# GpSimd's feature add moved behind VectorE's two-operand instructions, with both engines' rounds reordered

## The reference, cut to what matters

```python
xn = layernorm(x)
q, k, v = xn @ Wq, xn @ Wk, xn @ Wv            # 16 heads of 64
q, k = elu(q) + 1, elu(k) + 1
k_sum = k.sum(over the 2048 rows)              # per batch and head
kv = einsum('bhnd,bhne->bhde', k, v)
out = einsum('bhnd,bhde->bhne', q, kv) / (q . k_sum + 1e-6)
x = x + out @ Wo + bo
h = square(relu(layernorm(x) @ W_fc.T)); y = h @ W_proj.T
x = x + (spikes of a 5-step threshold neuron driven by y) / 5
```

## Time and profile before

| | us |
|---|---|
| median of 3 runs | 1173.32 (1172.75 to 1173.76) |
| span of the profiled execution | 1172.8 |
| TensorE busy in it | 1071.5 (91%) |
| VectorE busy | 1027.1 (88%) |
| ScalarE busy | 736.5 (63%) |
| GpSimd busy | 650.7 (55%) |

### The profile page before, as it was taken

One profiled execution on the slowest core, in us unless ns is written; L12 is line 12 of the kernel. 1 busy time (PEld: TensorE's weight loads), 2 busy tenths in 40 slices (PEclk: granted clock), 3 DMA queues, 4 the chain that ended last, 5 costly groups with the idle time before them and its releaser, 6 DMA issues.

```text
span 1172.8 us, 21946 instructions
## 1 busy us (share of the span) xinstructions
PE 1071.5 (91%) x6384; PEld 626.0 (53%) x6384; DVE 1027.1 (88%) x1873; ACT 736.5 (63%) x1219; POOL 650.7 (55%) x390
## 2 busy tenths in 40 slices
PE   5888888888888889898999999999999999999998
PEld 2333333333333337665666666666666666666666
DVE  7888988998898856999999899899899899899976
ACT  5565756665666565557766666666766657666653
POOL 3334333333333434448787768767777677677742
PEclk9999999999999999999999999999999999999999
DMA  3332226225222213444454544434434434434421
GB/s 103 105 89 67 55 70 159 68 55 124 73 67 56 54 45 64 84 92 95 100 105 96 109 90 103 102 85 106 108 81 101 107 90 97 101 91 97 86 54 37
DMA packets 261849, 101.63 MB, mean 87 GB/s; under 512 B 216592, under 2 KB 259728, under 8 KB 261776
## 3 DMA queue, kind: packets, MB, share of 16 engines
q1 hardware_dynamic: 261776, 100.84, 37.4%
HBM read 31.59 MB, written 16.78 MB: 41 GB/s over the span
## 4 chain that ended last, share of the span: by engine, by line
DVE 45%; PE 20%; issue 19%; ACT 15%; DVEq 1%; POOL 0%; ACTq 0%; DMA 0%
DVE xn L833 13%; ACT feat L668 6%; DVE feat L969 6%; ACT feat L666 6%; PE acc L599 5%; PE acc L578 5%; DVE zsum L972 5%; DVE feat L841 4%; PE proj L488 4%; PE acc L565 3%; DVE spikes L944 3%; DVE newt L827 2%; DVE newt L830 2%; ACT xnat L662 2%; DVE newt L824 2%
## 5 line engine op out<-in xcount | busy, mean ns | idle before, releaser
L1037 POOL TENSOR_TENSOR qT<-qT,feat 128x1024 f32<-128x1024 f32 x64 | 151.4, 2366 | 268.7 <-DVE feat L841 268.7
L1057 POOL TENSOR_TENSOR h<-h_f,h 128x512 f16<-128x512 f32 x128 | 145.8, 1160 | 157.0 <-ACT h L775 157.0
L511 PE MATMUL acc<-feat,xnat 128*128 128x512 f16 x768 | 176.9, 380 | 39.8 <-DVE feat L865 39.6
L488 PE MATMUL proj<-xn2T,xT 128*128 128x512 f16 x768 | 178.3, 382 | 33.2 <-DMA xT<-xnat 29.2
L841 DVE SCALAR_TENSOR_TENSOR feat<-proj,feat 128x1024 f32<-128x1024 f32 x128 | 156.4, 1222 | 56.3 <-ACT feat L668 38.4
L1052 POOL TENSOR_TENSOR feat<-feat 128x1024 f16<-128x1024 f32 x64 | 185.7, 2901 | 20.6 <-ACT feat L754 20.6
L599 PE MATMUL acc<-wpT,h 128*128 128x256 f16 x1536 | 181.2, 276 | 12.6 <-DVE spikes L944 12.6
L565 PE MATMUL acc<-m_all,qT 128*128 (+1 forms) x1536 | 179.8, 274 | 4.7 <-DMA qT<-feat 3.4
L662 ACT ACTIVATE xnat<-xn 128x256 f16<-128x256 f32 x128 | 53.2, 416 | 201.5 <-DVE xn L833 201.2
L578 PE MATMUL acc<-xn2T,wfcT 128*128 128x512 f16 x768 | 176.2, 379 | 0.0
L488 PE MATMUL proj<-wq,xT 128*128 128x512 f16 x768 | 176.2, 379 | 0.0
(11 more groups left out here) (56 smaller groups left out, 1337.0 us busy)
## 6 DMA issues: line engine op xcount, KB each, us to landing
x_t<-in_L_attn_x_dram SPq DMA_DIRECT2D x128, 128.0 KB, 2.2
xT_spill<-xT SPq DMA_DIRECT2D x64, 128.0 KB, 1.9
xT<-xT_spill SPq DMA_DIRECT2D x64, 128.0 KB, 2.1
out_dram<-out_t SPq DMA_DIRECT2D x64, 128.0 KB, 1.9
m_all<-in_L_attn_Wk_dram SPq DMA_DIRECT2D x4, 256.0 KB, 4.8
xT<-xnat SPq DMA_TRANSPOSE x64, 2.4
m_all<-in_L_ffn_W_fc_dram SPq DMA_DIRECT2D x4, 256.0 KB, 3.1
wv<-in_L_attn_Wv_dram SPq DMA_DIRECT2D x4, 256.0 KB, 3.3
```

Of the source, the lines that this page charges most:

```text
L488: mm = pe.matmul(proj[:, slot, half * HALF:(half + 1) * HALF], xT[:, u, left * C2 + c2, :], w[:, right, c2, half * HALF:(half + 1) * HALF] ...
L511: mm = pe.matmul(acc[:, c2 * 2 + half, :], xnat[:, u, left, c2 * P:(c2 + 1) * P], feat16[:, u % 2, right, half * HALF:(half + 1) * HALF], ...
L1037: pool.tensor_tensor(kacc[:, b, :], kacc[:, b, :], feat[:, u % 2, :], ALU.add).then_inc(k_added, 1)
L1057: pool.tensor_tensor(h[:, par, LO, f, :], h_f[:, f % 4, :], h[:, par, HI, f, :], ALU.subtract).then_inc(h_lo, 1)
```

## The change

The four parts belong together:

- GpSimd's add of tile n no longer starts when elu n is done. It waits as well for "ln1.lo" of tile n+3, that is for `xn_lo` of VectorE's round n+1.
- VectorE's round: three Newton steps n+2, statistics n+3, (g copies,) `xn` n+2, `k_lo` n-1, (split,) `xn_lo` n+2, elu n.
- ScalarE's round: `k_hi` n-1, (g copies,) `xn_hi` n+2, exp n, seed n+3, relu n+1, (split). Relu is thus one round ahead of its exp.
- The features of tiles u = 0, 1 of a chunk stay in `feat`; those of u = 2, 3 lie in the first half of `x2`. The waits for a free buffer reach back four tiles instead of two.

In front of the Q stage the waits on "k_lo" and "k_added" follow the new buffers, and VectorE waits for all adds before its chunks. GpSimd's loop leaves out the last chunk, which is written out so that its last waits can be constants.

```diff
+        def k_feat(u):
+            return feat[:, u, :] if u < 2 else x2[:, (u - 2) * HD:(u - 1) * HD]
...
+            def neg_part(slot, dst, neg):
+                act.activation(dst, proj[:, slot, :], ACT.Relu, scale=-1.0 / QK_SCALE).then_inc(neg, 1)
+
+            def exp_part(dst, neg, exp, count):
                 act.wait_ge(neg, count)
+                act.activation(dst, dst, ACT.Exp, bias=ln16[:, :], scale=-1.0).then_inc(exp, 1)
+
+            def k_neg_tile(c, u):
+                act.wait_ge(k_proj, 4 * c + u + 1)
+                wait_past(act, k_lo, 4 * c + u - 3)
+                wait_past(act, k_added, 4 * c + u - 2 if live(c, u - 4) else 0)
+                neg_part(u % 2, k_feat(u), k_neg)
 
             def k_exp_tile(c, u):
-                act.wait_ge(k_proj, 4 * c + u + 1)
-                wait_past(act, k_lo, 4 * c + u - 1)
-                wait_past(act, k_added, 4 * c + u if live(c, u - 2) else 0)
-                exp_part(u % 2, u, k_neg, k_exp, 4 * c + u + 1)
+                exp_part(k_feat(u), k_neg, k_exp, 4 * c + u + 1)
...
                 for u in range(4):
                     if live(*at(c, u - 1)):
                         k_hi_tile(*at(c, u - 1))
+                    if b and u == 1:
+                        copy_g(b - 1, (0, 1))
                     if live(*at(c, u + 2)):
                         xn_hi_a(*at(c, u + 2))
-                    if b and u == 1:
-                        copy_g(b - 1, (0, 1))
                     if live(c, u):
                         k_exp_tile(c, u)
                     if live(*at(c, u + 3)):
                         seed_rstd(ln1, *at(c, u + 3))
+                    if live(*at(c, u + 1)):
+                        k_neg_tile(*at(c, u + 1))
                     if b:
                         split_hi(b, u)
...
-            act.wait_ge(k_lo, TILES - 1)
-            act.wait_ge(k_added, TILES)
+            act.wait_ge(k_lo, TILES - 3)
+            act.wait_ge(k_added, TILES - 2)
             q_exp_tile(0, 0)
...
             def a_chunk(c, b):
                 for u in range(4):
-                    if live(*at(c, u + 2)):
-                        for _ in norm_a(*at(c, u + 2)):
-                            pass
+                    norm = norm_a(*at(c, u + 2)) if live(*at(c, u + 2)) else iter(())
+                    for _ in range(3):
+                        next(norm, None)
                     if live(*at(c, u + 3)):
                         stats_a(*at(c, u + 3))
+                    if b and u == 1:
+                        copy_g(b - 1)
+                    next(norm, None)
                     if live(*at(c, u - 1)):
                         k_lo_tile(*at(c, u - 1))
+                    if b and u:
+                        split_lo(b, u - 1)
                     if live(*at(c, u + 2)):
                         xn_lo(ln1, *at(c, u + 2))
-                    if b and u == 1:
-                        copy_g(b - 1)
-                    if b and u:
-                        split_lo(b, u - 1)
                     if live(c, u):
                         dve.wait_ge(k_exp, 4 * c + u + 1)
-                        elu_plus_one(u % 2, u).then_inc(k_elu, 1)
+                        elu_plus_one(u % 2, k_feat(u)).then_inc(k_elu, 1)
...
             q_elu_tile(0, 0)
+            dve.wait_ge(k_added, TILES + 1)
             chunks(dve, b_chunk)
...
+            def add_k(b, c, u):
+                pool.wait_ge(k_elu, 4 * c + u + 1)
+                pool.wait_ge(ln1.lo, 4 * c + u + 4 if live(c, u + 3) else TILES)
+                pool.wait_ge(k_added, 4 * c + u + 1)
+                pool.tensor_tensor(kacc[:, b, :], kacc[:, b, :], k_feat(u), ALU.add).then_inc(k_added, 1)
+
             for b in range(B):
-                with pool.Fori(b * BATCH_CHUNKS, (b + 1) * BATCH_CHUNKS) as c:
+                with pool.Fori(b * BATCH_CHUNKS, (b + 1) * BATCH_CHUNKS - (b == B - 1)) as c:
                     for u in range(4):
-                        pool.wait_ge(k_elu, 4 * c + u + 1)
-                        pool.wait_ge(k_added, 4 * c + u + 1)
-                        pool.tensor_tensor(kacc[:, b, :], kacc[:, b, :], feat[:, u % 2, :], ALU.add).then_inc(k_added, 1)
+                        add_k(b, c, u)
+            for u in range(4):
+                add_k(B - 1, CHUNKS - 1, u)
```

More of the change, by code:

```diff
@@ L662, in xn_hi @@
                 act.activation(xnat[:, u, HI, :], xn[:, u % 2, :], ACT.Copy).then_inc(ln.hi, 1)
-            def exp_part(slot, u, neg, exp, count):
-                act.activation(feat[:, u % 2, :], proj[:, slot, :], ACT.Relu, scale=-1.0 / QK_SCALE).then_inc(neg, 1)
+            def neg_part(slot, dst, neg):
+                act.activation(dst, proj[:, slot, :], ACT.Relu, scale=-1.0 / QK_SCALE).then_inc(neg, 1)
+            def exp_part(dst, neg, exp, count):
                 act.wait_ge(neg, count)
-                act.activation(feat[:, u % 2, :], feat[:, u % 2, :], ACT.Exp, bias=ln16[:, :], scale=-1.0).then_inc(exp, 1)
+                act.activation(dst, dst, ACT.Exp, bias=ln16[:, :], scale=-1.0).then_inc(exp, 1)
[4 more added lines that the diff above has]
+                neg_part(u % 2, k_feat(u), k_neg)
             def k_exp_tile(c, u):
-                act.wait_ge(k_proj, 4 * c + u + 1)
-                wait_past(act, k_lo, 4 * c + u - 1)
-                wait_past(act, k_added, 4 * c + u if live(c, u - 2) else 0)
-                exp_part(u % 2, u, k_neg, k_exp, 4 * c + u + 1)
+                exp_part(k_feat(u), k_neg, k_exp, 4 * c + u + 1)
             def k_hi_tile(c, u):
@@ L679, in k_hi_tile @@
                 wait_past(act, g_done, 4 * c + u - 1)
-                act.activation(feat16[:, u % 2, HI, :], feat[:, u % 2, :], ACT.Copy).then_inc(k_hi, 1)
+                act.activation(feat16[:, u % 2, HI, :], k_feat(u), ACT.Copy).then_inc(k_hi, 1)
             def copy_g(b, banks):
@@ L725, in _ @@
             seed_rstd(ln1, 0, 2)
+            k_neg_tile(0, 0)
             quads(act, a_chunk)
@@ L746, in q_exp_tile @@
                 wait_past(act, q_lo, 4 * c + u - 1)
-                exp_part(u % 2, u, q_neg, q_exp, 4 * c + u + 1)
+                neg_part(u % 2, feat[:, u % 2, :], q_neg)
+                exp_part(feat[:, u % 2, :], q_neg, q_exp, 4 * c + u + 1)
             def q_hi_tile(c, u):
@@ L837, in xn_lo, with elu_plus_one @@
                 dve.tensor_tensor(xnat[:, u, LO, :], xn[:, u % 2, :], xnat[:, u, HI, :], ALU.subtract).then_inc(ln.lo, 1)
-            def elu_plus_one(slot, u):
-                return dve.scalar_tensor_tensor(out=feat[:, u % 2, :], in0=proj[:, slot, :], scalar=QK_SCALE,
-                                                in1=feat[:, u % 2, :], op0=ALU.add, op1=ALU.max)
+            def elu_plus_one(slot, dst):
+                return dve.scalar_tensor_tensor(out=dst, in0=proj[:, slot, :], scalar=QK_SCALE,
+                                                in1=dst, op0=ALU.add, op1=ALU.max)
             def split_lo(b, i):
@@ L864, in k_lo_tile @@
                 dve.wait_ge(k_hi, 4 * c + u + 1)
-                dve.tensor_tensor(feat16[:, u % 2, LO, :], feat[:, u % 2, :], feat16[:, u % 2, HI, :],
+                dve.tensor_tensor(feat16[:, u % 2, LO, :], k_feat(u), feat16[:, u % 2, HI, :],
                                   ALU.subtract).then_inc(k_lo, 1)
@@ L954, in q_elu_tile @@
                 dve.wait_ge(q_exp, 4 * c + u + 1)
-                elu_plus_one(u % 2, u).then_inc(q_elu, 1)
+                elu_plus_one(u % 2, feat[:, u % 2, :]).then_inc(q_elu, 1)
             def q_steps(c, u):
```

## The result

The changed kernel takes 1103.91 us (median of 4 runs, 1103.69 to 1104.51) against 1173.54: a ratio of 0.9404, 95% interval 0.9389 to 0.9419. The forecast was 1103, range 1093 to 1122. The profiled span is 1101.9 instead of 1172.8, 70.9 less.

What follows compares the result with a forecast made beforehand. A loop of waits, with xn held by GpSimd's add, was taken to bound the K stage; 61 rounds falling from 396.6 to 327.4 us save 69.2, the tail 0.9, so 1172.8 becomes 1102.8, plus 0.5: 1103, range 1093 to 1122.

Steps and rivals of the forecast that it cites:

- (a): VectorE's xn in the K stage: the late add no longer holds it, gaining 1.50 us per round.
- rival 3: VectorE's elu is held by GpSimd's add: 6.7 us per round, 1185; chance 0.03 together with a clock fall.
- (c): K-stage rounds: all loops lie below 5.18 us, so TensorE sets the pace; smallest slack 1.0 us.
- The next loop: Loop through transpose, k_tile, relu, k_hi, k_lo and xn_lo: 9.4 us for two rounds, 4.7 each.
- Rival 1: A loop of 5.5 to 5.9 us takes TensorE's place; at 5.6, 25 us more, 1128; chance 0.16.
- (b): ScalarE does relu a round ahead, so relu leaves the loop of waits, which becomes about 4.5 us.
- the circle: K-stage loop of waits: xn, xn_hi, relu, exp, elu, next xn; 6.44 us per round before the change.
- (e): Extra waits at three batch starts, 6.9 us in all, SyncE's weight-turning rounds, 3, and filling at the start, 1.5.
- The start: Filling at the start of the K stage: 1.5 us added to the rounds.
- The tail: From elu 61 to the last g_tile: 13.8 us instead of 14.64, so 0.9 more saved.
- The sum: Elu 0 to elu 61: 61 × 5.18 = 316.0, plus 6.9, 3 and 1.5, is 327.4; 70 saved in all.
- Rival 4: TensorE's granted clock falls from 1.00; at 0.81 no gain; chance 0.03 together with elu being held.

Runs made afterwards that it cites:

- the smoothing: Changed kernel with xn, xn_hi ahead of batch-start g copies, weight splits two by two in rounds 2 and 3, weight halves turned two rounds apart: 1101.24 us, 0.9371.

## Why the prediction was right, step by step

- **xn is held by the add, 1.50 us per round (a).** Right, and shown by the add's removal: 1922 to 413 ns, and by the add's return to elu's end: a median of 1365 ns in the reordered rounds.
- **Elu isn't held, though the add starts ahead of it (rival 3).** Right: 1226 ns at most, with the add at 306.19 and elu at 306.63.
- **TensorE takes over at 5.18 (c).** Right: 304.94 to 310.12. The layout came true within 0.2: with k_tile at 0, relu was worked out at 2.87, k_hi at 3.9, k_lo at 4.99 and xn_hi at 5.45, and they stand at 2.79, 3.71, 4.80 and 5.38.
- **The next loop is at 4.7.** Right for plain rounds, 4.66 on the mean of four with TensorE's floor lowered. Rival 1, which needed a loop above 5.18, fell with the 5.18 us of the changed kernel's own rounds.
- **Relu ahead (b).** Worked out rightly as a relief of the circle, but I gave it weight that it hasn't got: with the late add the old circle, 4.94, would have been under TensorE's 5.18 too. Without the reorder the kernel is 2.5 us slower, which is not clear of noise; only with the smoothing is the difference (5.8) clear.
- **Places with less slack (e).** By how much TensorE's groups start later than 2.59 us after one another: 8.7 at the batch starts, where I had 6.9 (its waits there sum to 6.4; a group behind a wait of 1.06 starts 1.23 late, for example), and 2.4 at the weight transposes, where I had 3, nearly all of it in the first of the two chunks. The last split was not held by the add for 1.3: it waited for ScalarE, 2.14 in the batch shown.
- **The start.** Wrong in sign. I had 1.5 us on top of the rounds, but the first two rounds were shorter than 5.18: elu follows elu after 4.21 and 4.55 us, together 1.6 less. TensorE's wait of 1.72 at 19.28 is in them.

```profile
17.40 1.22 DVE L834 SCALAR_TENSOR_TENSOR feat<-proj,feat 128x1024 f32<-128x1024 f32 x1 [0.61 <-ACT feat L654]
...
21.61 1.22 DVE L834 SCALAR_TENSOR_TENSOR feat<-proj,feat 128x1024 f32<-128x1024 f32 x1
...
26.16 1.22 DVE L834 SCALAR_TENSOR_TENSOR x<-proj,x 128x1024 f32<-128x1024 f32 x1 [0.39 <-ACT x L654]
```

- **The tail.** Wrong in sign. I had 13.8 us from elu 61 (here at 342.89) to the last g_tile, it took 15.5, before 14.6. The term assumed TensorE in front of k_lo; with two adds one behind the other k_lo was held to 2.48 and the next one to 1.95, and TensorE waited 1.45.
- **The sum.** Worked out were 327.4 us from elu 0 to elu 61; they took 325.5 (17.40 to 342.89): 316.0 for the rounds, 11.1 for the places with less slack and 1.6 less for the start. The first elu came 0.8 later, the tail 1.7 longer than worked out, the part behind the K stage 1.5 shorter. The total was 70.9 in the spans against 70, from errors of 1 to 3 us that cancel. The last step, 0.5 us from the span to the median, was 2.0 here; each run of the changed kernel lies 1.8 above its own span. That the forecast met the median within 1 us is luck; the pace of the rounds, which is nearly all of the gain, is not.
- **Rival 4, the clock.** It fell: 1.00 in the K stage with TensorE busy 97%.

## What to carry to other kernels

```profile
295.00:300.00 5.00, 3.06 (x15) 1.00 0.26 65
300.00:305.00 5.00, 4.94 (x16) 0.66 0.27 74
```

```profile
195.00:200.00 5.00, 2.99 (x14) 1.19 (x13) 4.24 (x10) 4.72 (x8) 2.36 (x1) 1.00 0.31 82
200.00:205.00 5.00, 5.00 (x17) 1.94 (x16) 3.69 (x10) 1.09 (x3) 2.35 (x1) 0.66 0.28 73
```

```profile
200.82 2.76 PE L473 MATMUL proj<-xn2T,xT 128*128 128x512 f16 x12 [2.15 <-DMA xT<-xnat]
```
